# 284 matmuls on constants in attention's first wait and ahead of the maximum jobs of steps 0 to 4

## The chip, the core and the metric

The kernel runs on one core of a Trainium2 chip. The metric is the device time of that core in microseconds (us), lower is better. The engines are TensorE (PE in the profile; its weight loads are PEld), VectorE (DVE), ScalarE (ACT), GpSimd (POOL) and SyncE (SP), which issues the DMAs. TensorE's clock has two levels, 1.2 and 2.4 GHz; the profile gives the granted clock as a share of the full one, so 0.50 is 1.2 GHz.

## What is computed

```python
xn = layernorm(x)                       # x: 1 x 4096 x 256
s = attention_block(xn)                 # 16 heads of 16, causal, rotary; then an MLP of 1024
g = silu(expert_block(xn))              # 8 experts, capacity 512, fallback network
out = x + s * g

# inside attention_block, the part of this case
scores = einsum('bhqd,bhkd->bhqk', q, k) / sqrt(16)
scores = where(causal, -inf, scores)
attn_out = einsum('bhqk,bhkd->bhqd', softmax(scores), v)
```

## The kernel before

The kernel has three parts. `project_tokens` normalises the rows and makes q, k, v and the routing. `attend` does the causal attention. `networks` runs twice, for the experts and for the dense network. Only `attend` is touched.

`attend` cuts the 16 heads into 4 groups of 4 and the 4096 queries into 8 chunks of 512. One pair of group and chunk is a step: 32 steps, in group 0 with the chunks in rising order 0 to 7. A step needs the maximum of each row of scores before it can take exponentials, so each step is done twice. The *maximum pass* (`max_job`, `max_jobs`) makes scores with 128 queries on the partitions. One job is one matmul of 52 rows by up to 512 keys (line 842) into one of three PSUM banks (`MB + off % 3`), and VectorE reduces the bank to one maximum per row (line 1026). Jobs of the even head use the upper 64 rows of the array, those of the odd head the lower 64. On the diagonal, two jobs at a time get four small matmuls that hide later keys (line 853). The *second pass* works in units of 128 keys: `scores` (lines 898 and 904) in two pairs, exponentials on ScalarE (line 999), and `weigh` (line 919), the sum with V over four heads side by side, 32 columns of the array each.

Everything on TensorE runs in an order written out in the program. First all jobs of steps 0 and 1 (`AHEAD = 2`). Then the units of step after step, with maximum jobs of later steps between them; `max_pass_pace` says how many jobs are done after each unit. By its plan the 4 + 8 + 12 units of steps 0 to 2 take the jobs up to number 155, and the last job of step 4 (number 221) falls at the fourteenth of the 16 units of step 3. A step's first unit copies its maxima with ScalarE (line 978) into the rows of the queries; these copies mark the steps in the trace. Steps 0 to 4 have 12, 28, 44, 60 and 76 jobs; two further jobs, in steps 2 and 5, are counts for the routing, two full-height matmuls each (lines 499 and 500).

Each job waits until its bank has been reduced:

```python
if off > 2:
    pe.wait_ge(reduced, off - 2)
bank = MB + off % 3
```

Before its first job TensorE waits for the constants that GpSimd makes (`masks`, 16 steps), then for the first loads of queries (`q_in`) and of keys and values (`kv_in`). SyncE issues these loads when the projection has stored its results. `idb` is a 128 x 128 identity in bf16 among these constants; `PV` is the PSUM bank of the weighted sums.

Of the kernel before, what the change touches and what calls it, by code (L numbers as in the profile page):

```python
# [10 lines left out]
P = 128  # L11
# [6 lines left out]
TPC = CH // P  # L18
# [574 lines left out]
def diagonal_jobs(c):  # L593

    paired = TPC // 2
    wide = [(j, (t, t + 2), c) for j in range(paired) for t in range(2)]
    return wide + [(j, (h,), c) for j in range(paired, TPC) for h in range(HG)]


AHEAD = 2  # L600
COUNT_AT = (2, 5)
PREPARE, FIRST_SUMS = 26, 25
SEND_AT, SEND_EVERY = 8, 4
ORDER = ((0, 1, 2, 3, 4, 5, 6, 7), (0, 7, 1, 6, 2, 5, 3, 4), (4, 3, 5, 2, 6, 1, 7, 0), (7, 0, 6, 1, 5, 2, 4, 3))
# [42 lines left out]
def attend(nc, io, scratch, keep):  # L647
# [9 lines left out]
    steps = [(group, c) for group in range(NG) for c in ORDER[group]]  # L657
    LS = len(steps)
    units = [key_blocks(c) for _, c in steps]
    jobs = [[(j, (h,), kc) for kc in range(c) for j in range(TPC) for h in range(HG)] + diagonal_jobs(c) for _, c in steps]  # L660
    for i, m in enumerate(COUNT_AT):
        jobs[m].append((None, (), i))
# [10 lines left out]
    with ExitStack() as ctx:  # L673
# [10 lines left out]
        idb = sb("idb", [P, P], BF16)  # L684
# [3 lines left out]
        ps = ctx.enter_context(nc.psum_tensor("psB", [P, 8, CH], F32))  # L688
        PV, MB = 4, 5
# [11 lines left out]
        constants, send_rows, count, take_counts, choose, zero_row, sent, ZR = routing(nc, ctx, scratch, keep, reduced)  # L701
        counted = [j_base[m + 1] for m in COUNT_AT]
        zeros_row = ZR[:, :].rearrange("p (a n) -> p a n", a=1).broadcast_to([MROWS, 2 * CH // D, D])

        with nc.Block() as block:
            @block.sync
            def _(sp):
# [9 lines left out]
                def load_k(group, c):  # L717
                    w = group % 2
                    for t in range(2):
                        for r, _, a in TERMS:  # L720
                            sp.dma_start(KS[w][TILE * t + r:TILE * t + r + HD, :, c * CH:(c + 1) * CH].bitcast(F32),
                                         qk[a, 1, group, t, :, :, c * CH:(c + 1) * CH]).then_inc(kv_in[w][c], 16)
# [98 lines left out]

            @block.tensor
            def _(pe):
                def max_job(i, off, job):

                    j, hs, kc = job
                    if j is None:
                        pe.wait_ge(reduced, off - 2)
                        return count(pe, ps[:, MB + off % 3, :], kc)
                    group, c = steps[i]  # L830
                    w = group % 2
                    width = CH if kc < c else P * (j + 1)
                    if hs[0] == 0 and j == 0 and kc == 0:
                        pe.wait_ge(q_in[i % 4], 128 * (i // 4 + 1))
                    if hs[0] == 0 and j == 0:
                        pe.wait_ge(kv_in[w][kc], 112 * (group // 2 + 1) + (32 if kc == 0 else 0))
                    if off > 2:
                        pe.wait_ge(reduced, off - 2)
                    bank = MB + off % 3
                    for at, h in enumerate(hs):  # L840
                        rows, b = slice(TILE * (h % 2), TILE * (h % 2) + KROWS), h // 2
                        mm = nc.tensor.matmul(ps[:, bank, at * width:(at + 1) * width], QS[rows, i % 4, b, j * P:(j + 1) * P],  # L842
                                              KS[w][rows, b, kc * CH:kc * CH + width], start=(at == 0), stop=(kc < c))
                    return mm
# [10 lines left out]
                def max_jobs(i, at):  # L855

                    off = j_base[i] + at
                    j, _, kc = jobs[i][at]
                    single = j is None or kc < steps[i][1]
                    if at % 2 == 1 and not single:  # L860
                        return
                    if single:
                        max_job(i, off, jobs[i][at]).then_inc(maxed, 1)
                        return
                    both = jobs[i][at:at + 2]
                    for n, job in enumerate(both):
                        max_job(i, off + n, job)
                    for half in range(2):
                        for n, job in enumerate(both):
                            mm = hide_later_keys(off + n, job, half)  # L870
                            if half == 1:
                                mm.then_inc(maxed, 1)
# [60 lines left out]
                pe.sem_inc(ou_ready, 1)  # L933
                pe.sem_inc(pv_done, RING)
                pe.wait_ge(masks, 16)
                for m in range(AHEAD):
                    for n in range(len(jobs[m])):
                        max_jobs(m, n)
# [591 lines left out]
```

## Time and profile before

| | us |
|---|---|
| median of 3 runs | 2446.33 |
| the three runs | 2446.33, 2446.22, 2468.96 |
| the profiled execution | 2425.88 |
| its span, first to last instruction | 2424.1 |

All durations in the rows come from the profiled execution. Times of the timeline and of the windows are us from the start of its span. Matmuls are pipelined, and their ends in the trace are modelled, so a busy TensorE isn't TensorE at its peak; the distance from one start to the next tells more than a duration.

### The profile page before, as it was taken

Reading aid. Unit: us, or ns where it says so; the run is one execution under the profiler, and the core shown is the slowest. Engines: PE = TensorE matmul, PEld = TensorE weight load, DVE = VectorE, ACT = ScalarE, POOL = GpSimd, SP = SyncE. Lnnn points to the kernel's source line nnn. Section 1 sums busy time; section 2 is a strip of 40 time slices with the busy share of each in tenths; the row PEclk is TensorE's granted clock in tenths of the full one; section 3 lists DMA queues with packets and bytes.
Section 4 is the critical chain, followed back from the end, with each engine's and each line's share of the span. In section 5 each row is a group of like instructions: output and inputs, shape, how many; then the busy total and the mean of one; then the engine's idle time right before and its main releaser. Section 6 shows DMA issues by size and latency. Waiting matters only on the chain. (4 is left out here: it accounts for less than half of the span.)

```text
span 2424.1 us, 48735 instructions
## 1 busy us (share of the span) xinstructions
PE 2257.1 (93%) x18892; PEld 1361.1 (56%) x18892; DVE 1952.4 (81%) x3662; ACT 1509.4 (62%) x1791; POOL 211.6 (9%) x287
## 2 busy tenths in 40 slices
PE   0999995999999999999999999999999979998998
PEld 0898882444444444444444444444444348887887
DVE  8778774668999989899889989889888716667776
ACT  2444341445677778777777778788788875555343
POOL 2111101100200310000000000000000000000444
PEclk9999995558999989999999999999999999999999
DMA  5232338211000120210001121000200025542232
GB/s 137 87 118 94 131 111 135 65 32 32 11 11 1 54 68 1 64 33 11 20 11 33 32 57 45 18 20 1 29 21 4 3 82 162 158 130 81 78 95 78
DMA packets 137512, 142.65 MB, mean 59 GB/s; under 512 B 35920, under 2 KB 101072, under 8 KB 137200
## 3 DMA queue, kind: packets, MB, share of 16 engines
q1 hardware_dynamic: 134272, 131.91, 19.3%
q0 software_dynamic: 3072, 8.39, 1.0%
q8 instruction: 119, 1.95, 0.4%
q14 instruction: 49, 0.40, 0.1%
HBM read 88.17 MB, written 51.02 MB: 57 GB/s over the span
## 5 line engine op out<-in xcount | busy, mean ns | idle before, releaser
L1026 DVE TENSOR_REDUCE attn_MX<-psB 128x1 f32<-128x512 f32 (+3 forms) x2176 | 1333.9, 669 | 213.5 <-PE psB L842 118.9
L999 ACT ACTIVATE attn_PB<-psB 128x1024 f32<-128x1024 f32 (+3 forms) x1152 | 1076.0, 953 | 393.9 <-PE psB L898 324.2
L842 PE MATMUL psB<-KS,attn_QS 52*128 52x512 f32 (+3 forms) x1152 | 338.6, 461 | 36.9 <-DMA V<-v_rows 26.3
L919 PE MATMUL psB<-attn_PB,V 128*32 128x256 f32 (+4 forms) x4184 | 359.6, 418 | 0.0
L919 PE MATMUL psB<-attn_PB,attn_V 128*32 128x256 f32 (+4 forms) x3544 | 324.4, 438 | 0.6 <-ACT attn_PB L999 0.3
L898 PE MATMUL psB<-attn_QS,KS 52*128 52x512 f32 (+3 forms) x1152 | 311.3, 491 | 4.3 <-ACT attn_QS L978 4.3
L898 PE MATMUL psB<-attn_QS,attn_KS 52*128 52x512 f32 (+3 forms) x1152 | 275.9, 465 | 10.7 <-ACT attn_QS L978 7.2
L842 PE MATMUL psB<-attn_KS,attn_QS 52*128 52x512 f32 (+3 forms) x1152 | 280.1, 408 | 4.9 <-DVE attn_MX L1026 4.0
L842 PEld LDWEIGHTS psB<-KS,attn_QS 52*128 52x128 f32 x1152 | 193.5, 206 | 107.7 <-DVE attn_MX L1026 63.4
L898 PEld LDWEIGHTS psB<-attn_QS,attn_KS 52*128 52x128 f32 x1152 | 111.9, 185 | 240.9 <-ACT attn_PB L999 113.3
L898 PEld LDWEIGHTS psB<-attn_QS,KS 52*128 52x128 f32 x1152 | 126.5, 196 | 213.8 <-issue 140.4
L842 PEld LDWEIGHTS psB<-attn_KS,attn_QS 52*128 52x128 f32 x1152 | 170.4, 187 | 32.5 <-DVE attn_MX L1026 23.3
L919 PEld LDWEIGHTS psB<-attn_PB,V 128*32 128x32 f32 x4184 | 84.8, 111 | 135.4 <-issue 124.7
L919 PEld LDWEIGHTS psB<-attn_PB,attn_V 128*32 128x32 f32 x3544 | 70.3, 108 | 107.6 <-issue 89.7
L378 ACT ACTIVATE proj_HT<-psA,proj_SB 128x512 f32<-128x512 f32 x64 | 44.1, 689 | 112.8 <-PE psA L43 102.7
L978 ACT ACTIVATE attn_QS<-psB 4x1024 fp32r<-4x1024 f32 x64 | 65.0, 1016 | 58.9 <-PE psB L881 57.2
L1288 ACT ACTIVATE HT_dense<-ps_dense,B_dense 128x512 f32<-128x512 f32 x64 | 44.0, 689 | 87.2 <-PE ps_dense L43 87.2
L43 PE MATMUL ps_experts<-KS 128*128 128x512 f32 x384 | 90.4, 395 | 5.6 <-SPq L1132 5.6
L43 PE MATMUL ps_dense<-KS 128*128 128x512 f32 x384 | 91.2, 398 | 4.4 <-SPq L1124 4.4
L43 PE MATMUL ps_experts<-KS,HH_experts 128*128 128x256 f32 x256 | 75.4, 294 | 14.5 <-DVE Y_experts L1430 13.9
L43 PEld LDWEIGHTS ps_experts<-KS 128*128 128x128 f32 x384 | 72.8, 191 | 21.5 <-ACTq L1261 6.5
L43 PEld LDWEIGHTS ps_dense<-KS 128*128 128x128 f32 x384 | 73.3, 192 | 19.9 <-ACTq L1261 4.6
(232 smaller groups left out, 3095.5 us busy)
## 6 DMA issues: line engine op xcount, KB each, us to landing
W<-in_w SPq DMA_DIRECT2D x18, 1024.0 KB, 5.5
qk_parts<-proj_PT SPq DMA_DIRECT2D x32, 512.0 KB, 2.8
attn_QS<-qk_parts SPq DMA_DIRECT2D x192, 64.0 KB
v_rows<-proj_VA SPq DMA_DIRECT2D x32, 256.0 KB, 2.0
KS<-qk_parts SPq DMA_DIRECT2D x96, 64.0 KB, 4.1
attn_KS<-qk_parts SPq DMA_DIRECT2D x96, 64.0 KB, 2.8
XN<-in_x SPq DMA_DIRECT2D x8, 512.0 KB, 7.5
rows_by_place<-proj_ZR SPq DMA_DIRECT2D x32, 128.0 KB, 2.2
```

Of the source, the lines that this page charges most:

```text
L43: mm = nc.tensor.matmul(out, pick_l(lhs[l], b), pick_r(rhs[r], b), start=(at == 0), stop=(at == len(terms) - 1))
L378: nc.scalar.activation(HT[:, f % 4, :], ps[:, TB + f % 4, :], ACT.Gelu, bias=SB1[:, f:f + 1]).then_inc(h_act, 1)
L842: mm = nc.tensor.matmul(ps[:, bank, at * width:(at + 1) * width], QS[rows, i % 4, b, j * P:(j + 1) * P], KS[w][rows, b, kc * CH:kc * CH + ...
L898: mm = nc.tensor.matmul(ps[:, 2 * (s % 2) + t, r * P:CH], KS[w][rows, pair, kb * P:(kb + 1) * P], QS[rows, i % 4, pair, r * P:CH], start=T ...
L919: mm = nc.tensor.matmul(ps[32 * h:32 * (h + 1), PV, cols], V[w][:, kb, 32 * h:32 * (h + 1)], PB[:, u % RING, h, cols], start=(k == 0 and f ...
L978: nc.scalar.activation(QS[rows, i % 4, :, :], ps[rows, 2 * (s % 2):2 * (s % 2) + 1, :].broadcast_to([MROWS, 2, CH]), ACT.Copy).then_inc((r ...
L999: nc.scalar.activation(PB[:, u % RING, 2 * pair:2 * pair + 2, r * P:CH], ps[:, 2 * (s % 2):2 * (s % 2) + 2, r * P:CH], ACT.Exp, scale=HD * ...
L1026: nc.vector.tensor_reduce(MX[:, m % 4, first:first + 2 * n - 1:2, kc], ps[:, MB + off % 3, 0:n * w].rearrange("p (h n) -> p h n", h=n), AX ...
L1288: nc.scalar.activation(HT[:, f, :], ps[:, f % 4, :], ACT.Gelu, bias=bias).then_inc(h_act, 1)
```

## The change

`keep_busy(bank, n)` issues n matmuls of the identity with itself, repeated four times: 128 rows, 128 output rows, 512 columns, bf16. Their result lands in a PSUM bank and is overwritten by the next real matmul there, which starts a new sum. Sixty-four go to the bank `PV` between the wait for the constants and the first job. One goes ahead of each of the 220 jobs of steps 0 to 4, behind the job's wait for its bank and into that bank. Nothing else differs.

```diff
 AHEAD = 2
 COUNT_AT = (2, 5)
+ACCOMPANIED = 5
 PREPARE, FIRST_SUMS = 26, 25
...
             @block.tensor
             def _(pe):
+                def keep_busy(bank, n):
+
+                    for _ in range(n):
+                        nc.tensor.matmul(ps[:, bank, :], idb[:, :], idb[:, :].rearrange("p (a n) -> p a n", a=1).broadcast_to([P, TPC, P]),
+                                         start=True, stop=True)
+
...
                     if off > 2:
                         pe.wait_ge(reduced, off - 2)
                     bank = MB + off % 3
+                    if i < ACCOMPANIED:
+                        keep_busy(bank, 1)
                     for at, h in enumerate(hs):
...
                 pe.wait_ge(masks, 16)
+                keep_busy(PV, 64)
                 for m in range(AHEAD):
```

## Rows read from the trace of the kernel before

**Rows 1.** The page: busy time by engine; granted clock in 40 equal slices, in tenths.
```profile
PE 2257.1 (93%) x18892; PEld 1361.1 (56%) x18892; DVE 1952.4 (81%) x3662; ACT 1509.4 (62%) x1791; POOL 211.6 (9%) x287
...
PEclk9999995558999989999999999999999999999999
```

**Rows 2.** Windows: length, busy us (and instructions) of PE, PEld, DVE, ACT, POOL; clock; DMA.
```profile
363.70:387.80 24.10, 0.00 (x0) 0.01 (x1) 0.00 (x0) 0.00 (x0) 8.09 (x30) 0.50 0.71 123
416.40:565.10 148.70, 145.81 (x947) 64.74 (x947) 97.02 (x163) 67.46 (x77) 8.72 (x20) 0.51 0.17 43
565.10:583.20 18.10, 17.61 (x173) 9.01 (x169) 16.71 (x29) 11.13 (x11) 0.00 (x0) 1.00 0.01 2
490.00:493.40 3.40, 3.28 (x34) 1.66 (x29) 3.40 (x7) 2.23 (x3) 0.00 (x0) 1.00 0.00 0
599.30:602.70 3.40, 3.40 (x21) 0.87 (x20) 1.59 (x4) 1.01 (x2) 0.00 (x0) 0.50 0.79 185
660.00:840.00 180.00, 176.92 (x1710) 85.11 (x1707) 172.20 (x289) 130.37 (x136) 17.55 (x19) 1.00 0.07 20
```

**Rows 3.** Timeline (start, length, what): the last mask and the first attention matmul.
```profile
372.39 0.30 POOL L812 TENSOR_SCALAR_AFFINE_SELECT attn_later_kq<-attn_later_kq 64x128 bf16<-64x128 bf16 x1
...
387.82 0.48 PE L842 MATMUL psB<-KS,attn_QS 52*128 52x128 f32 x2 [26.32 <-DMA V<-v_rows]
```

**Rows 4.** Timeline of VectorE in the stretch of maximum jobs alone.
```profile
398.22 9.65 DVE L1026 TENSOR_REDUCE attn_MX<-psB 128x1 f32<-128x512 f32 x16
```

**Rows 5.** Timeline of ScalarE: copies of the maxima at the ends of steps 2 and 3.
```profile
522.26 2.05 ACT L978 ACTIVATE attn_QS<-psB 4x1024 fp32r<-4x1024 f32 x2
...
585.96 2.06 ACT L978 ACTIVATE attn_QS<-psB 4x1024 fp32r<-4x1024 f32 x2
```

**Rows 6.** Timeline of TensorE: full-height matmuls of 512 columns in the projections.
```profile
325.00 0.40 PE L43 MATMUL psA<-proj_WH,proj_NXL 128*128 128x512 f32 x1
325.24 0.40 PE L43 MATMUL psA<-proj_WH,proj_NXH 128*128 128x512 f32 x1
```

**Rows 7.** Windows at the starts of the two networks, from the first dense matmul on.
```profile
1978.20:1981.70 3.50, 3.50 (x9) 2.73 (x10) 0.00 (x0) 0.56 (x1) 0.00 (x0) 0.51 0.57 198
2222.00:2227.40 5.40, 5.32 (x13) 4.17 (x14) 3.75 (x11) 4.62 (x7) 3.35 (x4) 0.50 0.54 133
```

**Rows 8.** Window of the reductions (line 1026) alone: DVE busy, clock, DMA.
```profile
416.40:583.20 166.80, 110.86 (x181) 0.56 0.15 38
```

**Rows 9.** Timeline of TensorE: one unit at the half clock.
```profile
439.87 1.93 PE L919 MATMUL psB<-attn_PB,V 128*32 128x512 f32 x8
441.73 0.79 PE L898 MATMUL psB<-attn_QS,KS 52*128 52x512 f32 x2
442.33 0.63 PE L842 MATMUL psB<-KS,attn_QS 52*128 52x512 f32 x2
442.88 0.33 PE L919 MATMUL psB<-attn_PB,V 128*32 128x64 f32 x3
```

**Rows 10.** The same at the full clock.
```profile
623.71 0.39 PE L842 MATMUL psB<-KS,attn_QS 52*128 52x512 f32 x2
624.04 0.64 PE L919 MATMUL psB<-attn_PB,V 128*32 128x256 f32 x8
624.61 0.50 PE L898 MATMUL psB<-attn_QS,KS 52*128 52x512 f32 x2
624.94 0.44 PE L842 MATMUL psB<-KS,attn_QS 52*128 52x512 f32 x2
```

**Rows 11.** Timeline of TensorE around the second count job.
```profile
643.39 0.28 PE L499 MATMUL psB<-route_OVB,route_tri 128*128 128x256 bf16 x1
643.51 0.27 PE L500 MATMUL psB<-route_OVB,route_ones 128*128 128x256 bf16 x1
643.71 0.50 PE L898 MATMUL psB<-attn_QS,KS 52*128 52x512 f32 x2
```

## Prediction, made before the changed kernel ran

> **What bounds the kernel now.** I read the page first. TensorE is busy for 93% of the span, VectorE for 81%, and the row PEclk shows three slices at 5 where nearly all others show 9 [rows 1]. So I asked for busy times by stage, cut where the clock changes [rows 2]. From 363.7 to 565.1 us of the span the granted clock is 0.50, that is 1.2 GHz, with 3.4 us at 2.4 GHz in between; from 565.1 on it is back at 1.00. The reader is to see two different stretches in there. From 363.7 to 387.8 TensorE does nothing. The timeline shows why: its first attention matmul starts at 387.82, after 26.32 us of idleness, released by the DMA that loads V [rows 3]. The masks that it also needs are made by 372.7. From 387.8 to 416.4 only the maximum pass of steps 0 and 1 runs (40 jobs), and the clock doesn't bound it: sixteen reductions of 512 columns follow each other without a gap in 9.65 us, 0.60 us each [rows 4].
>
> From 416.4 on scores, weighted sums and maximum jobs are interleaved, and there the half clock costs time. VectorE is busy for 97.0 of 148.7 us, against 172.2 of 180.0 us later at the full clock [rows 2]. So TensorE bounds the first, and VectorE the second. The copies of the maxima mark the steps; step 3 lies between those at 522.26 and 585.96 [rows 5], so the cold stretch ends inside step 3.
>
> **The change part by part.** It removes and moves nothing. It adds 64 matmuls (call one K) behind the wait for the masks, and one K in front of each of the 12 + 28 + 44 + 60 + 76 = 220 jobs of steps 0 to 4. K is 128 rows by 512 columns and writes a bank that the next real matmul opens anew. A count job has none. No DMA, wait or semaphore is added; what stands behind a K is the rest of TensorE's queue.
>
> *The price of one K.* The nearest rows are full-height matmuls of 512 columns in a row: starts 0.23 us apart at the full clock [rows 6]. At the half clock 13 fit in 5.4 us and 9 in 3.5 us, 0.39 to 0.42 us each [rows 7].
>
> *The 64 in the wait.* They start at about 372.8, at the half clock. In the networks the clock rose 3.5 and 5.4 us after dense matmuls began [rows 7]. So 9 to 13 K run at half speed and 51 to 55 at 0.23 us: 372.8 + 3.5 + 12.7 = 389.0, or 372.8 + 5.4 + 11.7 = 389.9. The load is there at 387.8, so attention starts 1.2 to 2.1 us late; I take +1.7. If the clock didn't rise, 64 x 0.42 = 27 us would end at 399.7: 12 us late. If all ran full, 14.7 us: nothing late.
>
> *The 40 in front of steps 0 and 1.* A job with its K takes two times 0.23 to 0.31 us on TensorE, 0.46 to 0.62, under VectorE's 0.60 or level with it. In the jobs of the diagonal, K's 0.2 to 0.3 us comes ahead of matmuls that get shorter by as much. I take 0, with 2 us either way. If VectorE's cover were gone they would cost 40 x 0.27 = 11 us.
>
> *The other 180, from 416.4 to about 583.* From 416.4 to 583.2 VectorE makes 181 reductions [rows 8], so the last K falls at about 583. This stretch lasts 148.7 + 18.1 = 166.8 us now. First, what a full clock gives TensorE without any K. A full unit is two pairs of scores, four jobs and a weighted sum of 512 columns. Cold, starts lie 0.60, 0.55 and 1.86 us apart: 2 x 0.60 + 2 x 0.55 + 1.86 = 4.16 us [rows 9]. At the full clock 0.33, 0.33 and twice 0.57: 2.46 us [rows 10]. That is 0.59, so 148.7 us of cold time would be 88. The last 18.1 us are at the full clock already and bound by VectorE; TensorE alone would need about 16. Together 104. VectorE is busy for 97.0 + 16.7 = 113.7 us of it; at the later share of 172.2 / 180.0 = 0.957 that is 119 us, so without K the stretch would be 119.
>
> Then the K. Two jobs of neighbouring heads lie on different halves of the array and run at once: both start at 623.71 and the next work starts 0.33 us later [rows 10]. K takes all rows, so it parts them: K, job, K, job one behind the other. With a spacing of s between them and 0.33 behind the last, two jobs cost 3s more, one job 1.5s. What s is, the trace doesn't show for this order. It lies between 0.23 us, the spacing in the full-height stream [rows 6], and 0.31 us: where the shape of the tile changes, from a full-height matmul of 256 columns (L500) to the scores, the next start comes 0.20 us later, while the same matmul behind its like starts 0.12 us later [rows 11]; 0.08 us more on 0.23. I take 0.27, half way, as K's small bf16 weights should be ready early and the job's larger ones not. A job that stands alone pays about the same, since it keeps its own place and gains a K and one change of shape. (Three spacings over two jobs is 0.405 us a job.) 180 x 0.405 = 73 us, so 104 + 73 = 177 us: 10 us more than now. At s = 0.23: 104 + 62 = 166, 1 us less. At s = 0.31: 104 + 84 = 188, 21 us more.
>
> The Trainium skill has a rule here (TensorE: Matmul & The Clock Gate, Part 3, the mechanism): a weight load runs under a matmul only if their row groups differ; and a load of 128 columns is given as 128 / 1.2, 107 ns (Part 2). K shares row groups with every job, so s would be 0.213 + 0.107 = 0.32, the 180 K would cost 86 us and the stretch 190. The trace agrees where the shape changes [rows 11] and disagrees in the full-height stream, where 0.23 us leaves no room for a load [rows 6].
>
> **Sum.** +1.7 + 0 + 10 = +12 us on the profiled execution's 2425.9 us: 2438 us. The gain of the clock is real, 48 us if VectorE bound the stretch, but the K eat it. The timed runs before don't lie at 2425.9: they are 2446.2, 2446.3 and 2469.0, 20 and 43 us longer. A likely reason is the clock: it rose at 490.0 and fell again 3.4 us later, and rose for good at 565.1, in a stretch where nothing in the work changed [rows 2]; a run in which it rises later pays more. Work of 148.7 us cold would take 119 - 18 = 101 us at the full clock, so a cold us costs 0.32 us, and 20 us is some 60 us more of cold time. The K take that chance away, so I expect the changed kernel's runs at its own profiled level: 2438, 0.3% under the median of 2446.3.
>
> **Rivals.**
> - *The K fit into slack.* TensorE's ends are modelled, and its jobs do wait for VectorE here and there; K would fill those waits. The floor is VectorE's 119 us, a gain of 48: 2380. Half way between 166 and 119 it is 143 us, 24 less: 2404. For it: VectorE's share. Against it: TensorE shows 145.8 of 148.7 us busy [rows 2]. 0.18.
> - *Every change of shape shows its weight load*, s = 0.31: 188 us, +21 + 1.7 = 2449. For it the one row of L500; against it that K's load is short. 0.15. The skill's rule above says the same and a little more.
> - *The clock falls back* among the interleaved work and stays down (slower). Place: the short units at the seams of steps 1 to 3, as at 599.3, where it fell for 3.4 us [rows 2]. The stretch has 38 units (4 + 8 + 12 of steps 0 to 2 and 14 of step 3) of 4.75 jobs. Cold, a K costs its 0.43 us and some 0.27 for the pair it parts: 166.8 / 38 + 4.75 x 0.7 = 7.7 us a unit against 177 / 38 = 4.7. All 38 units: +115, 2553. From 11 units on it is slower by 1%. Against it: similar work without K held the full clock from 660 to 840 [rows 2]. 0.08.
> - *The excess of the timed runs is not the clock's* and stays: 2438 + 20 = 2458. For it: two of the runs agree to 0.1 us, which chance would not often do. 0.17.
>
> **How the numbers follow.** The forecast has 0.42, with a range of its own of 2424 to 2454. The range over all leaves out the lowest part of the slack case and the cold one: 2405 to 2462. This kernel's measurement tells about 1% from no change, so faster means under 2421.9 and slower over 2470.8. Faster: nearly all of the slack case and a little of the forecast, 0.21. Slower: the cold case, and the tails of the excess and of the weight loads, 0.14. Same: 0.65.
>
> **What would show it.** The clock row at 1.00 from about 378 on, with no 5 up to 600. The first attention matmul at 389 to 390. The mark at 522.3 stays within some 10 us of its place, and up to it VectorE is busy for about two thirds of the time; a share that low at the full clock says that the K bind. K to job 0.23 or 0.31 apart. After 600 the same times as before, shifted. Wrong if VectorE is at 95% from 418 on (slack), if any stretch shows 0.50 with K in it, or if the changed kernel's runs lie 20 us over its own profile.

## The result and the profile after

The changed kernel is slower by 8%. Four runs of it took 2628.97, 2626.58, 2637.34 and 2655.32 us, median 2633.15; before, 2446.27. The ratio is 1.0815, with a 95% interval of 1.0704 to 1.0927. The prediction said 2438 us, range 2405 to 2462. A ratio leaves out the executions that lie over 1.5% above the fastest of their kernel, which here cuts into the spread that every one of these kernels has, so medians over all executions are given as well where that matters.

The page of the changed kernel (its execution of 2628.97 us): the span, busy time by engine, and the clock in 40 slices.

```profile
span 2627.2 us, 49303 instructions
...
PE 2478.9 (94%) x19176; PEld 1417.0 (54%) x19176; DVE 1964.3 (75%) x3662; ACT 1509.3 (57%) x1791; POOL 211.3 (8%) x287
...
PEclk9999995555559899899999999999999999999999
```

Where [rows 1] has three slices at 5, this has six, and the slices are longer. The windows of the changed kernel, cut where the clock changes (columns as in [rows 2]):

```profile
372.30:375.70 3.40, 3.40 (x9) 1.19 (x9) 0.00 (x0) 0.00 (x0) 2.93 (x7) 0.51 0.55 128
375.70:388.00 12.30, 12.30 (x58) 5.41 (x56) 0.00 (x0) 0.00 (x0) 0.31 (x2) 1.00 1.01 140
388.00:399.50 11.50, 11.40 (x58) 5.19 (x57) 7.60 (x16) 0.00 (x0) 0.00 (x0) 1.00 0.83 163
399.50:432.40 32.90, 32.54 (x86) 11.96 (x86) 16.41 (x28) 0.00 (x0) 0.00 (x0) 0.50 0.49 80
432.40:785.30 352.90, 350.67 (x1361) 121.33 (x1361) 129.31 (x204) 84.84 (x94) 8.73 (x20) 0.50 0.07 18
785.30:850.00 64.70, 63.38 (x597) 30.33 (x597) 62.08 (x104) 43.77 (x48) 9.37 (x22) 1.00 0.15 35
```

The reader is to see three things. The 64 K in the wait do what they are there for: after 3.4 us of them the clock is at 1.00, and it stays there until 399.5. Then it falls, in the middle of jobs that all have a K in front, and for 385.7 us it doesn't come back, though TensorE is busy for 350.7 of 352.9 us. It comes back at 785.3, 13 us after the start of the last K at 772.3. (That distance isn't fixed: in the second profiled execution of this kernel it was 30 us, and 48 us in the kernel without the 64, below.) VectorE, 97.0 of 148.7 us before [rows 2], is busy for 129.3 of 352.9.

The maxima are copied for the first time at 432.43 (416.46 before), and for the fourth and fifth time here (the changed kernel's ScalarE; of before, [rows 5]):

```profile
634.75 2.06 ACT L988 ACTIVATE attn_QS<-psB 4x1024 fp32r<-4x1024 f32 x2
...
778.79 2.06 ACT L988 ACTIVATE attn_QS<-psB 4x1024 fp32r<-4x1024 f32 x2
```

So 16 us of the loss are made before the first mark, and 352.9 - 166.8 = 186 us between it and the end of the K. What follows is untouched: from 583.2 to its end before takes 1840.8 us of its span, from 785.3 to its end (2627.2) the changed kernel takes 1841.9. 16 + 186 = 202, and the spans differ by 203.1.

Now one job and its K at the half clock, and below at the full clock. Start, length, engine (PEld is the weight load), what:

```profile
600.50 0.11 PEld L828 LDWEIGHTS psB<-attn_idb 128*128 128x128 bf16 x1 [0.44 <-issue]
600.51 0.61 PE L828 MATMUL psB<-attn_idb 128*128 128x512 bf16 x1
...
601.05 0.29 PEld L851 LDWEIGHTS psB<-KS,attn_QS 52*128 52x128 f32 x1 [0.44 <-issue]
601.05 0.79 PE L851 MATMUL psB<-KS,attn_QS 52*128 52x512 f32 x1
601.77 0.10 PEld L828 LDWEIGHTS psB<-attn_idb 128*128 128x128 bf16 x1 [0.44 <-issue]
601.77 0.61 PE L828 MATMUL psB<-attn_idb 128*128 128x512 bf16 x1
```

```profile
397.93 0.39 PE L828 MATMUL psB<-attn_idb 128*128 128x512 bf16 x1
...
398.24 0.18 PEld L851 LDWEIGHTS psB<-KS,attn_QS 52*128 52x128 f32 x1 [0.23 <-issue]
398.25 0.49 PE L851 MATMUL psB<-KS,attn_QS 52*128 52x512 f32 x1
...
398.67 0.39 PE L828 MATMUL psB<-attn_idb 128*128 128x512 bf16 x1
```

In these rows every weight load begins only when the other matmul's columns have had their time, and the matmul's start is put down at the start of its load. At the half clock K to job is 0.54 us, which is 0.43 of columns (512 at 1.2 GHz) and 0.11 of K's load, and job to K is 0.72, which is 0.43 and 0.29 of the job's load: 1.27 us for a job with its K (600.50 to 601.77). At the full clock it is 0.32 and 0.42, together 0.74.

### The profile page after: what moved, and what is told of

Read it like the earlier page. It is cut to its first block and busy times, and to the rows that moved or that the text cites. A ratio compares the mean times of both kernels' runs of the same rounds, so it can differ in the third digit from the quotient of the medians.

```text
span 2627.2 us, 49303 instructions
## 1 busy us (share of the span) xinstructions
PE 2478.9 (94%) x19176; PEld 1417.0 (54%) x19176; DVE 1964.3 (75%) x3662; ACT 1509.3 (57%) x1791; POOL 211.3 (8%) x287
## 5 line engine op out<-in xcount | busy, mean ns | idle before, releaser
L851 PE MATMUL psB<-KS,attn_QS 52*128 52x512 f32 (+3 forms) x1152 | 406.5, 483 | 5.8 <-DVE attn_MX L1036 2.6
L928 PE MATMUL psB<-attn_PB,V 128*32 128x256 f32 (+4 forms) x4184 | 369.8, 429 | 0.0
L907 PE MATMUL psB<-attn_QS,KS 52*128 52x512 f32 (+3 forms) x1152 | 322.0, 504 | 4.3 <-ACT attn_QS L988 4.3
L851 PEld LDWEIGHTS psB<-KS,attn_QS 52*128 52x128 f32 x1152 | 207.7, 208 | 140.2 <-issue 100.8
L828 PE MATMUL psB<-attn_idb 128*128 128x512 bf16 x284 | 145.9, 552 | 11.6 <-POOL attn_later_kq L813 11.3
L828 PEld LDWEIGHTS psB<-attn_idb 128*128 128x128 bf16 x284 | 29.5, 104 | 102.4 <-issue 54.5
```

What stands on the lines that cost most here:

```text
L828: nc.tensor.matmul(ps[:, bank, :], idb[:, :], idb[:, :].rearrange("p (a n) -> p a n", a=1).broadcast_to([P, TPC, P]), start=True, stop=True)
L907: mm = nc.tensor.matmul(ps[:, 2 * (s % 2) + t, r * P:CH], KS[w][rows, pair, kb * P:(kb + 1) * P], QS[rows, i % 4, pair, r * P:CH], start=T ...
L928: mm = nc.tensor.matmul(ps[32 * h:32 * (h + 1), PV, cols], V[w][:, kb, 32 * h:32 * (h + 1)], PB[:, u % RING, h, cols], start=(k == 0 and f ...
```

## The experiments

Two facts on the kernel before come from the 62 executions of it that ran beside the experiments. They took 2389.1 to 2474.4 us, median 2433.5, with mean granted clocks of 0.972 down to 0.924. Time and clock lie on a line (correlation -0.995): 17.4 us for each 0.01 of the clock. A single execution therefore says something only together with its clock.

**Only the 64.** Was it the wait, or the jobs?

```diff
-                    if i < ACCOMPANIED:
-                        keep_busy(bank, 1)
```

> Only the 64 matmuls on constants in the wait stay; no job has one in front. Theory A (the loss comes from the matmul in front of each job: between two tiles of different height both weight loads stand in the open, 0.10 us for K and 0.18 to 0.28 us for the job, and TensorE streams too little to keep the full clock): the clock rises at 376 as in the changed kernel, falls again once the thin stretch of maximum jobs has begun, near 395, and from there all is as before; 2425 to 2450 us. Theory B (the 64 shift the loads or the buffers and the loss follows from that): over 2500 us. A gain of over 1% would say that a warm start carries into the interleaved stretch.

Eleven runs had a median of 2445.3 us beside 2450.6 of before; ratio 1.0034, interval 0.993 to 1.0138. The profiled execution, at 2492.4 us and a clock of 0.917 the longest of the eleven, shows the clock rising at 376 and falling at 392.7, once the jobs have begun; then it is cold until 656, with 3.4 us in between:

```profile
375.70:392.50 16.80, 15.60 (x88) 7.45 (x86) 3.75 (x8) 0.00 (x0) 0.17 (x1) 1.00 0.98 126
392.70:414.90 22.20, 19.82 (x73) 10.25 (x72) 18.89 (x36) 0.03 (x1) 0.00 (x0) 0.50 1.03 175
414.90:585.00 170.10, 167.33 (x1072) 73.71 (x1076) 110.35 (x184) 76.43 (x86) 8.74 (x20) 0.51 0.15 37
585.00:656.00 71.00, 71.00 (x428) 28.20 (x420) 45.74 (x75) 32.04 (x35) 0.00 (x0) 0.50 0.11 27
```

As theory A said, the clock that the 64 bring is gone before the interleaved work begins. Whether they cost or gain anything within the interval isn't shown. These rows also say something that matters for the argument. With no K in front of any job the clock fell 7 us earlier than in the changed kernel, and behind the first mark it stayed down through 184 + 75 = 259 of VectorE's instructions, where the changed kernel's cold stretch has 204. It is one execution of each, but it shows that a half clock that lasts through so much of the work needs no K. What K one by one did was to fail to lift it, and to make the work at the half clock longer.

**Only the K in front of jobs.**

```diff
-                keep_busy(PV, 64)
```

> Only the matmul in front of each job of steps 0 to 4 stays; the 64 are gone. Theory A: the whole loss is here, 2615 to 2660 us, the clock at 0.50 from 364 to where the last K stands, near 780. Theory B: as before, under 2470 us.

One run, 2642.0 us, the clock at 0.50 from 365 to 826. The whole loss is here; theory B falls.

**Real data in K.** An identity is nearly all zeros.

```diff
-nc.tensor.matmul(ps[:, bank, :], idb[:, :], idb[:, :].rearrange("p (a n) -> p a n", a=1).broadcast_to([P, TPC, P]),
+nc.tensor.matmul(ps[:, bank, :], keep["XN"][:, 2, 0:P].bitcast(BF16)[:, 1::2],
+                 keep["XN"][:, 0:2, :].bitcast(BF16)[:, :, 1::2],
```

> The changed kernel, but K multiplies rows of the normalised input (bf16 halves of XN, as weights and as moving data) instead of an identity. Theory A: nothing changes, the clock is at 0.50 from 400 to 780, 2615 to 2660 us. Theory C (a matrix that is nearly all zeros doesn't count as activity for the clock): the clock stays at 1.00 from 376 on and the time is under 2500 us.

2583.3 us, cold from 405 to 664. Neither theory had that: the clock wasn't held, but it came back while K were still being issued.

```profile
405.00:664.00 259.00, 256.68 (x974) 90.65 (x973) 97.10 (x154) 55.44 (x64) 8.72 (x20) 0.50 0.16 34
664.00:732.00 68.00, 68.00 (x425) 26.78 (x423) 40.35 (x64) 24.60 (x26) 0.00 (x0) 1.00 0.00 1
```

It rose at 664.5, in the middle of step 3, and stayed at 1.00 until 746.4; the last K starts at 728.5. So here one K in front of every job went with a full clock for 64 us. The stretch also gives the price of K at the full clock. Step 3 takes 144.0 us in the changed kernel, all of it cold (634.75 to 778.79). Here it takes 29.5 us cold and 68.3 at the full clock (634.97 to 732.77), so 68.3 us stand for the other 114.5: a factor of 0.60. By it the changed kernel's 352.9 us would be 210 at the full clock, an estimate.

The kernel was timed, and then timed again beside the changed kernel.

> The changed kernel with real data in K once more, timed. Its one execution took 2583 us, the changed kernel 2627 to 2655 in four, with the clock back at 664 instead of 785. Theory C in a weak form (fewer zeros count for more): its median stays under 2610 us. If data don't matter: 2610 to 2660 us, and the 2583 is one end of a spread.

> The changed kernel itself, beside the next on one chip. If data matter (theory C, weak): its median lies 30 us or more over that of the kernel with real data. If not: within 15 us of it.

> The changed kernel with real data in K, beside the run before this. Theory C, weak: median 2570 to 2600 us. No effect of data: 2620 to 2650 us.

Four runs took 2546, 2584, 2599 and 2626 us, median 2591.8, as the weak form of theory C had it. Beside each other on one chip, real data had 2500, 2625, 2630 and 2636, median 2627.7, and the changed kernel 2628, 2631, 2645 and 2648, median 2637.8: 10 us apart, which by the terms set before is no effect. In all, nine executions with real data lie between 2500 and 2636, and five of them under 2600, while eight of the changed kernel all lie in 2627 to 2655. Were the data of no account, all five would fall on the side of the real data in some 2 of 100 cases (an estimate: five drawn from seventeen). Data may let the clock come back sooner now and then. They aren't the whole cause, since a profiled execution with real data was cold from 399 to 798 too. What share they have stays open.

**K of the job's own kind.**

```diff
                     if i < ACCOMPANIED:
-                        keep_busy(bank, 1)
+                        rows, b = slice(TILE * (hs[0] % 2), TILE * (hs[0] % 2) + KROWS), hs[0] // 2
+                        nc.tensor.matmul(ps[:, bank, :], QS[rows, i % 4, b, j * P:(j + 1) * P],
+                                         KS[w][rows, b, kc * CH:(kc + 1) * CH], start=True, stop=True)
```

> The changed kernel, but in front of each job stands a matmul of the job's own kind: the same 52 rows, the same weights, 512 columns. No change of tile height is left. If it is the change of height that bares the weight loads (theory A1), the start of K and that of its job are 0.43 us apart at the half clock and two heads overlap again, a job with its K costs under 0.6 us and the time is 2420 to 2500 us. If it is that both use the same rows of the array (theory A2), the job starts 0.6 to 0.7 us after its K, two heads still overlap in part, and the time is 2480 to 2600 us.

One run, 2424.7 us at a clock of 0.968. Its timeline at the half clock (L853 is the job, L849 the matmul in front of the next):

```profile
404.06 0.62 PE L853 MATMUL psB<-KS,attn_QS 52*128 52x512 f32 x1
404.06 0.79 PE L849 MATMUL psB<-KS,attn_QS 52*128 52x512 f32 x1
404.65 0.62 PE L853 MATMUL psB<-KS,attn_QS 52*128 52x512 f32 x1
404.66 0.79 PE L849 MATMUL psB<-KS,attn_QS 52*128 52x512 f32 x1
```

A job with such a matmul takes 0.60 us at the half clock, where it doesn't wait for VectorE, less than half of the 1.27 with K: it runs beside the job of the other head, on the other half of the array. This clock fell in the thin stretch as well (392 to 433) and came back 13 us after the first mark; it wasn't down for the 385.7 us of the changed kernel. Theory A1 holds: the same 512 columns in front of every job cost little when the tile's height doesn't change. By the line above, though, a run of before at a clock of 0.968 takes about 2394 us, so these matmuls still cost some 30, by estimate. And since K's changes of height are gone here, they aren't what makes the clock fall in the thin stretch.

**K in front of the 40 jobs of steps 0 and 1 alone.**

```diff
-ACCOMPANIED = 5
+ACCOMPANIED = 2
```

> The changed kernel with K in front of the 40 jobs of steps 0 and 1 alone (and the 64 in the wait). Theory A: the stretch of maximum jobs alone ends where it did in the changed kernel (first step mark at 432 instead of 416), since there a job with its K takes 1.26 us at the half clock against VectorE's 0.60; from there on all is as before, so 16 us over a run of before with as much cold clock, 2420 to 2485 us. If the loss sat in the first wait or in these 40, the time would stay over 2550 us.

2443.8 us, first mark at 431.5, clock 0.951. From there to 600 the clock is at 0.74 on the mean, which no K touches. It was as expected: 15 us in the thin stretch, and the big loss sits in the 180 K behind it.

**K of 128 columns.** How much of the price is columns?

```diff
-                        keep_busy(bank, 1)
+                        nc.tensor.matmul(ps[:, bank, 0:P], idb[:, :], idb[:, :], start=True, stop=True)
```

> The changed kernel, but K in front of a job streams 128 columns instead of 512. In the changed kernel a K costs the interleaved stretch (353 - 155) / 180 = about 1.1 us at the half clock. Streaming alone is 0.43 us of it. Theory A (the weight loads stand in the open and pairs are parted): 0.32 us less per job with K, so 220 x 0.32 = 70 us less than the changed kernel, 2540 to 2590 us, and job to next K still 0.7 us. Theory D (it is the columns that cost): three quarters of the loss goes, 2470 to 2510 us.

2596.5 us, cold from 395 to 777. First to fifth mark take 288.6 us (426.3 to 714.9); in the changed kernel 346.4 (432.4 to 778.8). The difference, 58 us over the some 180 K in there, is 0.32 us each, exactly three quarters of the columns at 1.2 GHz. The other two thirds of the price stayed. Theory D, columns alone, falls. The total is a little over the expected range, since this execution had some 47 us more of cold time after 1000 (97 against 50) than the changed kernel's profiled one. The clock came back 68 us after the last K (708.8).

**Two K in front of every second job.** As many K, half the changes of height.

```diff
-                    if i < ACCOMPANIED:
-                        keep_busy(bank, 1)
+                    if i < ACCOMPANIED and (off - j_base[i]) % 2 == 0:
+                        keep_busy(bank, 2)
```

> The changed kernel with as many K, but two of them in front of every second job and none in front of the other. Half as many changes of tile height, and two neighbouring jobs can overlap again. Theory A: per two jobs 0.43 + 0.54 us for the K and 0.28 us for the bared load behind, instead of 2.1 us, so 180 / 2 x 0.85 = 75 us less than the changed kernel, 2530 to 2580 us at the same clock, less if the clock comes back sooner. Theory D: the same columns, the same time, 2615 to 2660 us.

> The kernel with two K in front of every second job once more, timed. Theory A (the clock is what all is about, and it holds here): every execution has a granted clock of 0.97 or more, 2400 to 2430 us, a spread under 30 us where before has 75. If the one execution seen was luck: a spread like that of before or the changed kernel, up to 2600 us.

The first run took 2421.8 us: some 210 us less than the changed kernel, with the same number of K. That is far more than the 75 that the weight loads could give. The clock did it:

```profile
377.00:418.00 41.00, 37.22 (x210) 15.91 (x207) 24.46 (x47) 4.20 (x4) 0.00 (x0) 0.99 0.99 156
418.00:428.00 10.00, 10.00 (x47) 4.13 (x46) 4.84 (x8) 2.53 (x5) 0.00 (x0) 0.51 0.08 18
428.10:585.90 157.80, 157.80 (x1268) 61.13 (x1268) 113.79 (x185) 74.06 (x83) 8.77 (x20) 1.00 0.14 37
```

It is at 1.00 but for 10 us, and still the marks gain hardly anything on before: the fourth stands at 515.97 (522.26 before) and the fifth at 585.89 (585.96 before). VectorE is busy for 113.8 of 157.8 us, so TensorE bounds the stretch at the full clock, by the K. Timed, ten runs had a median of 2440.6 us, 2429 to 2471, and a ratio of 1.0125, interval 1.0081 to 1.0169. The clock was 0.960 to 0.985. The spread is 42 us against 84 of before in the same sitting. The expectation was missed in time, spread and clock; the kernel is slower than before by 1.3%, clear of noise. The profiled one of the ten, at 2450.1 us, was at 1.00 from 426.3 to 583.7 as well; its clock fell behind the last K, from 596 to 637.

**Two K in front of every job.** The test that parts clock from price: 220 K more than the changed kernel has.

```diff
-                        keep_busy(bank, 1)
+                        keep_busy(bank, 2)
```

> The changed kernel with two K in front of every job: 220 more than it has. Theory E (the loss is the half clock, which comes from one K alone between two jobs; two K in a row stream densely enough to hold the full clock): the clock is at 1.00 through most of 390 to 700, a job with its two K takes 0.23 + 0.32 + 0.42 = 0.97 us, the interleaved stretch 104 + 180 x 0.80 = 248 us instead of 353, and the time is 2490 to 2550 us: faster than the changed kernel with twice its K. Theory D (the K themselves cost): at the half clock every further K adds 0.43 us, 2700 to 2740 us.

2521.7 and 2550.8 us: over 80 us *less* than the changed kernel, with 504 K against its 284. The windows of the first:

```profile
431.00:448.00 17.00, 17.00 (x58) 5.31 (x56) 5.53 (x8) 3.72 (x6) 0.00 (x0) 0.50 0.04 12
448.20:679.50 231.30, 231.30 (x1443) 82.11 (x1442) 118.37 (x185) 74.10 (x83) 8.74 (x20) 1.00 0.10 25
```

and its timeline at the full clock:

```profile
562.00 0.60 PE L828 MATMUL psB<-attn_idb 128*128 128x512 bf16 x2
562.54 0.50 PE L851 MATMUL psB<-KS,attn_QS 52*128 52x256 f32 x2
562.97 0.61 PE L828 MATMUL psB<-attn_idb 128*128 128x512 bf16 x2
```

Two K take 0.54 us to the next job, so the second costs 0.22. From first to fifth mark 251.5 us pass (428.0 to 679.5); 248 were expected. Theory E's forecast of the time and of the clock stands. Its reason, that one K alone brings the half clock, isn't shown: the run with real data held the full clock with one.

**Fewer K.** If two in a row hold the clock, how seldom may they come? In steps 0 and 1 still at every second job, then in front of every fourth or every eighth.

```diff
+                    if i < ACCOMPANIED and (off - j_base[i]) % (2 if i < AHEAD else 4) == 0:
+                        keep_busy(bank, 2)
```

> Two K in front of every second job in steps 0 and 1, and in front of every fourth job in steps 2 to 4: 90 K less than with two by two. If two K in a row this often still hold the full clock, the interleaved stretch gets shorter by half the price of the K, and the fourth copy of the maxima, 586 with two by two, comes near 568: 2395 to 2410 us, and little spread. If not, stretches at 0.50 appear between 430 and 570 and the time is 2405 to 2450 us.

> The same with every eighth job in steps 2 to 4. If the clock holds: near 560, 2385 to 2400 us. If it doesn't: as in the run with a dense entry, cold again from 460 to 500 on in most executions, 2390 to 2450 us.

Every fourth: the fifth mark at 564.5 and a full clock from 441 to 772 in the profiled execution, near the 568 that were expected (the expectation calls this mark the fourth), but a median of 2436.5 over ten runs, where 2395 to 2410 were expected; ratio 1.0041, interval 0.9989 to 1.0092: no difference from before. Every eighth: cold from 399 to 495 in the profiled execution, 2413 to 2513 us in four runs, no gain either.

**A version meant to gain.** The 64 stay; the jobs of steps 0 and 1 get a matmul of their own kind; twelve K stand where TensorE waits for ScalarE's first copy; nothing in front of any later job.

```diff
-                    if i < ACCOMPANIED:
-                        keep_busy(bank, 1)
+                    if i < AHEAD:
+                        rows, b = slice(TILE * (hs[0] % 2), TILE * (hs[0] % 2) + KROWS), hs[0] // 2
+                        nc.tensor.matmul(ps[:, bank, :], QS[rows, i % 4, b, j * P:(j + 1) * P],
+                                         KS[w][rows, b, kc * CH:(kc + 1) * CH], start=True, stop=True)
...
                 max_rows(0, 0, None, 1)
+                keep_busy(PV, 12)
```

> A version meant to gain: the 64 in the wait stay, the 40 jobs of steps 0 and 1 get a matmul of their own kind in front (as in the run with own tiles, 4 us), twelve K in a row stand between the maxima of step 0 and its first scores, and no later job has anything in front. Theory A with a clock that holds once it is up at the start of the interleaved work: first mark near 420, clock at 1.00 from about 425 on, step 3 ends near 560 instead of 586, 2390 to 2425 us. If the interleaved work of steps 0 to 2 cannot hold the clock by itself: cold again within 10 to 50 us of the mark, 2425 to 2465 us, no difference from before.

> The kernel with own tiles in steps 0 and 1 and twelve K before the first scores, timed again in more rounds. Its first ten executions had a median of 2410 beside 2427 of before. If that stands: a ratio of 0.988 to 0.997. If it was chance: 0.997 to 1.005.

In its first profiled execution the clock rose at 418 and fell again at 466, and was cold to 602; in the second it held:

```profile
389.00:419.90 30.90, 29.04 (x120) 18.73 (x121) 21.87 (x42) 2.19 (x3) 0.00 (x0) 0.50 0.82 139
420.10:543.20 123.10, 119.27 (x1151) 58.31 (x1151) 112.63 (x193) 77.19 (x88) 8.79 (x20) 0.99 0.18 49
```

Here the fifth mark is at 543.2, 43 us ahead of before, with VectorE at 91%: the gain of the clock that the prediction had put at 48. Over all executions the medians are 2410.5 beside 2427.0, and 2406.5 beside 2433.4; over both, the means of 22 and 30 executions are 2410.9 and 2426.0, 15 us apart with an uncertainty of about 11 (twice the standard error). The ratios, 0.9966 (0.9897 to 1.0036) and 1.0016 (0.997 to 1.0061), show no difference. The two go together if the version makes the good case more frequent and not the best case better: its fastest execution took 2385.2 us, that of before 2389.1. That the best executions of before have an early rise of the clock is likely by their clocks of 0.97, but none of them was profiled. It is the one version that points under before, by some 0.6%, and this isn't secured by the ratios.

## Why the prediction was wrong

**The start** was right to about 1.5 us. Attention's first matmul starts at 388.02 instead of 387.82; I had 389.0 to 389.9. The clock rose some 3.5 us into the K, as in [rows 7], and the K then ran about 0.22 us apart.

**The 40 jobs** I costed at nothing, under VectorE's 0.60 us. A job with its K takes 0.74 us at the full clock and 1.27 at the half, so TensorE took over as the bound, and the first mark came 16 us late. While the clock was up, fifteen K started in 11.5 us; at that pace the forty would have ended near 418, 2 us late. The other 14 are the half clock's. The cover was thinner than I said at either clock.

**The spacing s** was mis-sized. I took 0.27 between 0.23 and 0.31; measured are 0.32 and 0.42, 0.37 on the mean. My upper end came from [rows 11], which show only the way from a full-height matmul to the 52 rows of a score; there 0.31 was nearly right. For the way back, job to K, I had no row, and gave it the same value; it measured 0.42. What the runs show: where the height changes, the whole load stands in the open, 0.10 us for K and 0.18 us for the job at the full clock, 0.11 and 0.29 at the half. At the full clock this alone would have made the 180 K cost (0.74 - 0.17) x 180 = 103 us instead of 73, so 104 + 103 = 207 against 166.8; the run with real data gives 210 by its stretch at the full clock. With the start, the 2 us of the forty jobs and 40 to 43 here that is some 2470 us with the clock up: over the range by under 10 us, and no more. The run with two K each, expected by the same sum at 248 us and measured at 251.5, confirms its frame.

The rule that I had weighed (the Trainium skill, TensorE: Matmul & The Clock Gate, Part 3, the mechanism: a load runs under a matmul only if their row groups differ) was nearer than my number. The trace agrees for K and job, which share rows. It disagrees for two K in a row, 0.22 us apart, and in part for jobs with a matmul of their own kind, where the job's load runs while the matmul on the same rows is under way (a pair is 0.60 us apart at the half clock, 0.43 of it columns); so height, or the shape of the tile, parts the cases here, not the rows alone.

**The clock** was the step that failed. My sum had the full clock from 378 on, and 104 us of work without K rests on it. I held that the K would keep it, gave its fall 0.08, and placed that at the seams of steps 1 to 3. It fell at 399.5, in the plainest part, behind the third of sixteen jobs of full width each with its K, and was down for 385.7 us, through all the K that were left. At the half clock each of the 180 K costs about 1.0 us: the work without K, 148.7 us and 18.1 / 0.59 = 31, would take 179, and 352.9 - 179 = 174 over 180. The parts are 0.43 for its columns, 0.11 and 0.29 for the two loads, and 0.16 for the parted pair of jobs (0.43 alone instead of 0.27), 0.99 together. In the rival I had said 0.7 us a K, without the loads. Against the kernel before, which was cold there too, the 186 us of this stretch are these 174 and some 13 for the last 18.1 us, which were at the full clock before. Against the kernel that I predicted, the K at a full clock would account for some 2 + 43 of the loss of 203 us, and the half clock for the rest, near 158 (an estimate from the factor of 0.60). From first to fifth mark the run with two K each takes 251.5 us where the changed kernel takes 346.4, and carries more K.

**The slack case** was wrong: next to nothing was hidden. TensorE bounds at both clocks; at the full one, in the run with real data, it is busy for 68.0 of 68.0 us and VectorE for 40.4.

**The excess of the timed runs** is the clock's, as argued: the spread of before follows it at 17.4 us per 0.01, which is some 0.36 us for each cold us; I had 0.32. The remedy wasn't: in the changed kernel the mean clock is 0.90 to 0.91, where before has 0.92 to 0.97.

Shown, then: where the loss sits (the runs with one part each), the bared loads (the rows; own kind against K; 128 columns), and that the clock decides over 100 us of it (two each, two by two, and the stretch with real data at the full clock). Open is why the clock stayed down with one K in front of each job, while it came back within 10 to 17 us of its fall with two in a row at every or every second job. The bared loads are one candidate, since there is more of them per column with one K than with two. Against them as the whole reason stand two rows: with a matmul of the own kind the clock fell in the thin stretch as well, at 392, and with real data one K per job went with the full clock for 64 us. No run measures the loads, the columns and the data apart.

## What to carry to other kernels

A matmul of another height between two real ones bares both weight loads: here 0.57 us a job at the full clock and 1.0 at the half, where its columns alone are 0.21 and 0.43. If such matmuls are wanted, two in a row are the cheaper form (the second costs 0.22), and a matmul of the shape around it is cheaper still. None of the forms tried here is shown to gain; the full clock that two by two held was paid for in full by the K. Before adding them, ask what TensorE's time would be with them at *both* clocks: a stretch bound by another engine at the full clock leaves little room. A forecast that rests on a full clock needs a price for the case that it doesn't come. Where a kernel's runs spread, plot time against the granted clock before reading any single run. The version with dense work where TensorE waits anyway, and nothing in front of the later jobs, is the only one that points under before, and it isn't secured.

## What the hardware showed beyond that

- A TensorE that is busy all the time isn't a sign of the full clock: it was busy for 350.7 of 352.9 us, and the clock stayed at 0.50. The same pattern, one K per job, was at 1.00 for 64 us in the run with real data.
- The second of two full-height matmuls in a row costs 0.22 us; the first after a job costs 0.32, the job after it 0.42.
- The same kernel spreads over 85 us, and its time follows the mean clock (correlation -0.995). The clock comes back at another place in each execution: with real data at 664, 798 and 805 us in three profiled executions of one kernel, and in the version meant to gain it fell at 466 in one and held in the other.
